# A decoder layer on one core: the high and low halves of the attention context made earlier in a step

## What is computed

```python
x = x + _L0_attn_ref(_layernorm(x, axis=-1), Wq, Wk, Wv, Wo, bo)
x = x + _L0_xattn_ref(ctx_2048, ctx_2048, _layernorm(x, axis=-1), ssm_kernel, D, 8)
x = x + _L0_ffn_ref(_layernorm(x, axis=-1), w_gate_up, w_proj)
...
    q = _rope((h @ Wq).reshape(N, S, 32, 64).transpose(0, 2, 1, 3))
    k = _rope((h @ Wk).reshape(N, S, 8, 64).transpose(0, 2, 1, 3))
    v = (h @ Wv).reshape(N, S, 8, 64).transpose(0, 2, 1, 3)
    scores = (q @ k^T + alibi) / sqrt(64)
    scores = 30.0 * jnp.tanh(scores / 30.0)
    probs = softmax(where(causal, scores, -inf))
    ctx = (probs @ v).transpose(0, 2, 1, 3).reshape(N, S, 2048)
    return ctx @ Wo + bo
```

## Time and profile before

| | |
|---|---|
| median of 3 runs | 1187.93 us (1187.45 to 1189.96) |
| the profiled execution | 1186.55 us, span 1184.8 us |
| TensorE busy (PE) | 1131.4 us, 95% |
| VectorE busy (DVE) | 881.1 us, 74% |
| GpSimd busy (POOL) | 687.7 us, 58% |
| ScalarE busy (ACT) | 553.0 us, 47% |

### The profile page before, as it was taken

One profiled execution on the slowest core, in us unless ns is written; L12 is line 12 of the kernel. 1 busy time (PEld: TensorE's weight loads), 2 busy tenths in 40 slices (PEclk: granted clock), 3 DMA queues, 4 the chain that ended last, 5 costly groups with the idle time before them and its releaser, 6 DMA issues. The chain is left out here.

```text
span 1184.8 us, 27046 instructions
## 1 busy us (share of the span) xinstructions
PE 1131.4 (95%) x10882; PEld 810.0 (68%) x10882; DVE 881.1 (74%) x1287; ACT 553.0 (47%) x617; POOL 687.7 (58%) x557
## 2 busy tenths in 40 slices
PE   4998999989999999999899999999999999999998
PEld 4665566747657667576576677777886876786683
DVE  6979778787888787888877788888745645654654
ACT  6866564653755655637555500000244543542441
POOL 1454394784865947848659589999342422423331
PEclk9998999999999999999999999999999999999999
DMA  9463444563455355634455357783001022013000
GB/s 325 152 210 108 121 132 118 166 173 118 124 160 174 105 142 157 186 113 141 132 174 156 146 114 144 146 145 83 1 19 44 11 55 54 17 36 54 19 19 36
DMA packets 166183, 134.15 MB, mean 113 GB/s; under 512 B 69628, under 2 KB 127362, under 8 KB 166082
## 3 DMA queue, kind: packets, MB, share of 16 engines
q1 hardware_dynamic: 141128, 126.44, 37.3%
q10 hardware_dynamic: 24960, 6.29, 3.6%
HBM read 81.76 MB, written 35.21 MB: 99 GB/s over the span
## 5 line engine op out<-in xcount | busy, mean ns | idle before, releaser
L701 PE MATMUL bank<-hT_halves,w_hi 128*128 128x256 f16 x640 | 176.6, 276 | 13.5 <-DMA hT_halves<-parts 8.3
L1984 POOL TENSOR_TENSOR parts<-parts 128x512 f32<-128x512 f32 x80 | 118.2, 1480 | 107.6 <-DVE parts L1446 107.6
L702 PE MATMUL bank<-hT_halves,w_hi 128*128 128x256 f16 x640 | 176.3, 276 | 0.0
L703 PE MATMUL bank<-hT_halves,w_lo 128*128 128x256 f16 x640 | 176.3, 275 | 0.0
L963 PE MATMUL bank<-kv,toep 128*128 128x288 f32 (+2 forms) x660 | 157.8, 401 | 0.7 <-ACT qT L1211 0.5
L963 PEld LDWEIGHTS bank<-kv,toep 128*128 128x128 f32 x660 | 123.7, 190 | 34.0 <-ACT qT L1211 0.7
L2002 POOL TENSOR_TENSOR ctx_lo<-ctx,ctx_hi 128x512 f16<-128x512 f32 x64 | 105.7, 1652 | 67.2 <-ACT ctx_hi L1153 67.1
L1989 POOL TENSOR_SCALAR_AFFINE_SELECT region_c<-region_c 128x512 f32<-128x512 f32 x128 | 106.2, 854 | 60.2 <-ACT region_c L1177 60.2
L2132 POOL TENSOR_TENSOR sqsum<-sqsum,toep 128x512 f32<-128x512 f32 x56 | 78.1, 1395 | 95.4 <-ACT toep L1353 95.2
L1174 ACT ACTIVATE region_c<-bank,cap_scale 128x1536 f32<-128x1536 f32 x64 | 98.7, 1542 | 63.0 <-PE bank L782 62.9
L1041 PE MATMUL bank<-odd_halves,guT 128*128 128x256 f16 x512 | 112.2, 273 | 0.0
(11 more groups left out here) (192 smaller groups left out, 2633.9 us busy)
## 6 DMA issues: line engine op xcount, KB each, us to landing
unit_halves<-halves SPq DMA_DIRECT2D x80, 256.0 KB, 2.2
q_both<-unit_halves SPq DMA_DIRECT2D x64, 256.0 KB, 2.9
q_high<-unit_halves SPq DMA_DIRECT2D x64, 128.0 KB, 3.0
toep<-kernel_padded SPq DMA_DIRECT2D x32, 256.0 KB, 4.1
wffn<-w_gu SPq DMA_DIRECT2D x6, 1280.0 KB, 6.2
cpair<-ctx_pairs SPq DMA_DIRECT2D x32, 176.0 KB, 4.7
xin<-x SPq DMA_DIRECT2D x8, 512.0 KB, 3.8
region_o<-wq SPq DMA_DIRECT2D x4, 1024.0 KB, 11.5
```

Of the source, the lines that this page charges most:

```text
L701: pe.matmul(dst, lh, rh, start=first and k == 0, stop=False)
L702: pe.matmul(dst, lh, rl, start=False, stop=False)
L703: mm = pe.matmul(dst, ll, rh, start=False, stop=last and k == n - 1)
L1984: pool.tensor_tensor(slot[:, 0], slot[:, 0], slot[:, 1], ALU.add).then_inc(unit_summed, 1)
```

## The change

Two engines get another order; TensorE's, VectorE's and SP's lists are the same as before, and no instruction is added or removed.

ScalarE's `high_ctx(s - 3)` stands ahead of `soften(s)` in its step instead of behind it. GpSimd's `low_ctx` takes group s - 3 in step s instead of group s - 4, and stands behind `add_keys` instead of ahead of it. After the loop one `low_ctx` is left instead of two. The same is done in the list of the last batch.

```diff
@@ scalar, attend(b); the same move in last_batch()
                     if step == CUT_SLOT:
                         act.wait_ge(quant_step, QUANT_STEPS * (b - 1) + DIGITS)
+                    if step >= 3:
+                        high_ctx(b, step - 3, False)
                     if step < NG:
                         soften(b, step)
                     if step < TT:
                         take_values(b, step)
-                    if step >= 3:
-                        high_ctx(b, step - 3, False)
@@ gpsimd, attend(b); the same in last_batch()
                 for step in range(STEPS):
-                    if step >= 4:
-                        low_ctx(b, step - 4)
                     if 1 <= step < NG + 1:
                         add_keys(b, step - 1)
+                    if step >= 3:
+                        low_ctx(b, step - 3)
                     if 2 <= step < 2 + LATE:
                         add_parts(b, EARLY + step - 2)
...
-                for g in range(STEPS - 4, NG):
+                for g in range(STEPS - 3, NG):
                     low_ctx(b, g)
```

## The result

The changed kernel took 1194.2 us, the median of 20 runs (1189.57 to 1203.57). The kernel before took 1187.99 us in 20 runs beside them (1182.68 to 1190.33). The ratio is 1.0062 (95% interval 1.0046 to 1.0079): slower by 0.6%, against a forecast of 1194.3 us. The total came out at the forecast, but in good part by luck: the profile shows that its parts did not come as forecast.

The account below looks back on a forecast made before the run. TensorE, busy 95%, was taken as held at batch ends by hT, bound by the weights' load ahead of it. Six batches by +1.2 (+7.2) and the last batch -0.8 gave +6.4 us: 1194.3 us, range 1184 to 1199.

Parts of the forecast that it names:

- Add_parts(9) 1.15 late: GpSimd, batch 2: two low_ctx instead of one ahead of add_parts of unit 9, which starts 1.15 us late.
- L1594 0.9 to 1.5 late, taken as 1.2: VectorE's last quantisation step, ahead of the store and load, ends 0.9 to 1.5 us late per batch; 1.2 taken.
- The reading of the port: VectorE and GpSimd lock their shared port for a whole instruction; without that lock the sum is +6.1, not +6.4.
- the two cases for L1594: L1594 gets in after the first of mask(5)'s two instructions, ending at 248.55, or waits for the second, ending at 249.15.
- Rstd 1.75 late and the data 0.3 late: Batch 2: GpSimd's rstd comes some 1.75 us later, the standardisation ahead of hT's data starts only 0.3 late.
- Ctx_lo's waits vanish: TensorE's waits for ctx_lo, 8.8 us in batches 1 to 6 and 3.7 in the last, fall to under 2.
- The tanh costs nothing: ScalarE, step 6: tanh ends later, at 248.8, but 0.95 us of slack remains before scores(7); late-tanh rival 0.13.
- Waits for hT of about 24 us: TensorE's waits at the batch ends grow from 8.3 us by 6 x 2.7, to about 24 us.
- From load to hT a constant 12.3 us, so hT 1.2 later in each batch: hT stays 12.3 us behind the issue of the weights' load, so it moves 1.2 us in six batches: +7.2.
- The order on the queue: Descriptors of one queue on one DMA engine start in order, so transposes behind the loads cannot start before them.
- The round trip of the stores: From L1594 through the store to the load of weights: store and load move by the same 1.2 us as L1594.
- The last batch -0.8: Batch 7: nothing becomes late, TensorE saves between 0 and 3.7 us of ctx_lo waits; 0.8 taken.

Follow-up runs that it names:

- the low half behind: Changed kernel, but GpSimd's low_ctx stands behind add_parts and the deviation instead of ahead of them: 1183.4 us, 0.9973 of the kernel before.
- the second profile: The changed kernel run and profiled once more, nothing altered: 1198.41 us, 1.0087 of the kernel before.
- the short load: Changed kernel and kernel before, each loading only one of five w_gu tiles per share: 1183.89 us (0.9979) and 1183.92 us (0.9971).
- ScalarE's half: Kernel before with only the edit of ScalarE's list, GpSimd's list as before: 1188.8 us, 1.0014.
- the late load: Kernel before with an unused 128x896 VectorE reduction directly ahead of L1594: 1202.78 us, 1.0124.
- the quantisation moved: Changed kernel with scale_digits called in steps 1, 2 and 4 instead of 2, 4 and 5: 1192.87 us, 1.0039 of the kernel before.

## Why the prediction was right, and where it was not

- **Add_parts(9) 1.15 late: 0.86.** The way was right: an extra low_ctx ahead of it, and no gap to hold it (0.86 to 0.90 in the batches that began alike). Add_parts(8) came 0.87 late and not 0.95, and add_keys(3) ended 0.2 sooner than I had placed it.
- **L1594 0.9 to 1.5 late, taken as 1.2: 0.9.** The lower bound. The reading of the port held: add_keys(4) runs to 247.16, and L1592, which starts at 245.95, ends 1.9 us after that (3.10 us); low_ctx(2) takes 2.94 us beside it. Of the two cases for L1594 the number is that of the first, but the way was the second: it waited for both instructions of mask(5), to 251.24, and ended 1.88 us after that; it was no later because it had started 0.45 us sooner than I had placed it. The Trainium skill (SBUF — State Buffer, "SBUF: two separate sides") calls this an exclusive lock; the trace agrees, and in the kernel with the low half behind L1594 ends 1.89 us after the add_keys that stands in its way for 0.13 us (2.02 us).
- **Rstd 1.75 late and the data 0.3 late: 1.0 late, and the data 0.3 sooner.** L1417 stands behind normalise(5), and that came sooner, since TensorE's sums did.
- **Ctx_lo's waits vanish: right**, to the last of the 12.5 us.
- **The tanh costs nothing: right.** Tanh(6) ends at 252.94, and scores(7) start at 254.58, without a wait.
- **Waits for hT of about 24 us: 20.6 and 21.7.** Near, but not by the sum that gave the 24: see the next point.
- **From load to hT a constant 12.3 us, so hT 1.2 later in each batch: this step failed.** In batches 3, 5 and 6 the distance shrank to 11.0, 11.0 and 10.8 us, which I had named as a sign of the prediction being wrong. In batches 1, 2 and 4 it was 12.35, 12.12 and 12.45, behind a slow store, with the transposes issued only 4.2 to 4.6 us behind the load; in batch 1 they landed 6.3 to 7.0 us after their issue, against 2.9 to 3.7 before. The sum until hT is +3.1 us (+4.9 in the second profile), not +7.2. What is constant is another distance. The last load ahead of the transposes is that of the residual x (`xres`, L465), and the second transpose lands 1.8 to 2.0 us after it, in 10 of the 12 batches of the profiles before and after (3.3 in batch 1 after, 4.7 in batch 6 before), and never sooner. Its rows in batch 3, before and after (size, us from issue to landing):

```profile
xres<-x SPq DMA_DIRECT2D x1, 512.0 KB, 9.0
```

```profile
xres<-x SPq DMA_DIRECT2D x1, 512.0 KB, 7.4
```

It landed 10.3 us behind the issue of the load of weights before, and 9.0 us after. So my 12.3 us were some 10.3 + 1.9 and no fixed price: in batches 3 and 5 the residual landed 1.3 and 1.0 us sooner behind the load than before, and hT followed it; in batch 6 (8.8 and 8.9 us) the slow second transpose of before was gone. This isn't hT bound by its data alone either: it came 3.6 us behind its data there, and 3.0 with the short load, so the loads still held it for 0.6 us. Why the residual lands sooner in some batches isn't shown. It does explain why the distance from the load to the transposes doesn't decide alone: in the second profile's batch 1 it was 6.46, but the residual landed 10.2 us behind the load, and hT came at 12.22.
- **The order on the queue: right, but it is no constant.** No transpose landed ahead of the residual in either profile, which bears the order out better than the 12.3 us that I had put beside it.
- **The round trip of the stores was taken as fixed.** It was not in the sum, and cost 3.9 us over the six batches: 6.15, 5.88 and 6.25 us from L1594 to the load in batches 1, 2 and 4, where only batch 2 had such a one before.
- **The clock was not in the sum at all: +6.5 us (+7.1 in the second profile).** TensorE's idle time was gathered from small waits in the middle of a batch into one wait at its end. Behind each of the waits of 4.3 us and more in the two profiles the first matmuls run at a granted clock of 0.50, and the way to the next scores takes 30.46 us or more instead of 28.79. In batches 3, 5 and 6, with waits of 1.9 to 2.1 us, it is 28.79. I had counted a moved wait as worth its length.
- **The last batch -0.8.** From its first scores to the end it is +2.1. TensorE works at its half clock for 6.8 us there (669.6 to 673.0 and 843.7 to 847.1), and for none before; at half of that length this is worth 3.4 us, an estimate. That leaves about -1.3, between my 0.8 and the bound of 3.7. TensorE now waits 2.1 + 0.7 us at L860, the transposes of the x2 that the prediction named, in place of the 3.7 for ctx_lo.

So the side is right for the reason given: low_ctx ahead of add_parts(9), and so a late L1594 and load, is shown by the kernel with low_ctx behind, and by the short load. The size is right by luck: +7.2 for hT, where +3.1 was measured, and nothing for the clock, where it was some 5 in the medians and 6.5 in the profile, were two errors of opposite sign that about cancelled.

**Open** stays why the store's round trip takes 6 us in some batches and 4.0 to 4.8 in others, and with it which batches lose. It goes with the late L1594: the changed kernel has three slow ones of six in each of its two profiles and again with the short load, and the kernel before has one of six, batch 2, in its own profile, with the short load and with ScalarE's half. What links the two isn't shown. Open are also the residual's landing at 9.0 or at 10.3 us, the single slow transposes, and why they are more when TensorE is kept busy.

## What to carry to other kernels

Ahead of an instruction that begins a chain of DMA round trips, even one more short instruction on a busy engine is too much (1.16 us of low_ctx made L1594 0.9 us late); it can go behind, though what waits for its product then waits again. A wait taken out of the middle must be followed to the end of the stage, and a few short waits that come together in one long one can cost more than their sum, since TensorE's clock can fall behind it. A constant distance in the only profile there is (12.3 us from the load to hT) is not yet a price: look for what lands in between, and shorten one of the suspects.

## What the runs showed of the hardware

- TensorE's granted clock was 0.50 behind all of the waits of 4.29 to 5.28 us (nine, in four profiles), each a time in which TensorE did nothing; in one of them it fell 0.3 us after the wait. Behind shorter ones it varied: full behind 2.82 us in the kernel before and 3.08 with the low half behind add_parts, 0.50 behind 2.84 with ScalarE's half alone and 3.43 with the late load, and with the quantisation moved it fell 0.6 us after a wait of 2.22. It cost 1.7 to 2.9 us each in the changed kernel.
- A transposing DMA of the same size landed in 2.7 to 7.4 us, by what was ahead of it on its queue: a median of 2.8 us with one tile of five in the load, 3.9 with the whole load in the kernel before, and 5.0 with the whole load nearer to it. With the whole load, the second of the two landed 1.8 to 2.0 us after the last load ahead of it in 10 of 12 batches before and after the change, and never sooner.
- Two engines on the shared port: a low_ctx that takes 1.16 us alone took 2.94 beside VectorE's L1592, and L1592 took 2.45 to 3.10 us, by who was there first.
